# Squares of t summed on ScalarE in nine operations, the low part of h moved to VectorE, and new call orders on four engines

## The reference, cut to what matters

```
x = x + conv_block(ln_over_channels(x))      # 3x3 patches against 512 prototypes
t = tokens(x)                                # 96 channels each
t = t + ffn(ln_t(t))                         # 96 -> 384 -> 96, values rounded to fp8/fp16 steps
ln_t(v) = (v - mean(v)) / sqrt(var(v) + 1e-5)
```

## Time and profile before

| | |
|---|---|
| median of 3 runs | 1996.17 us (1995.54 to 1996.33) |
| the profiled execution | 1996.22 us, of which span 1994.4 us |
| busy, share of the span | PE 95%, DVE 94%, ACT 83%, POOL 81% |
| granted PE clock | 0.985 in the mean, 1.00 from 100 to 1900 us |
| DVE sum of squares (L1041) | 133.4 us in 128 operations |
| ACT squares (L510) | 119.6 us in 128 operations |
| POOL low part of h (L420) | 58.6 us in 128 operations |

### The profile page before, as it was taken

How to read it: one execution, slowest core, us unless ns; L and a number is a source line. 1 busy time by engine, 2 the same in 40 slices (tenths; PEclk the granted TensorE clock), 3 DMA queues, 4 the chain that set the end, 5 groups by cost and what they waited for, 6 DMA issues and landing times.

```text
span 1994.4 us, 44820 instructions
## 1 busy us (share of the span) xinstructions
PE 1898.1 (95%) x13105; PEld 1429.9 (72%) x13105; DVE 1866.6 (94%) x6525; ACT 1656.4 (83%) x3205; POOL 1621.8 (81%) x1170
## 2 busy tenths in 40 slices
PE   5899999999999999999999999999999999999964
PEld 3567777777777777777777777777777777777642
DVE  7999999999999999999999999999999999999740
ACT  1168888888888888888888888888888888888885
POOL 2578888888888888888888888888888888888752
PEclk9999999999999999999999999999999999999985
DMA  3324545454454545445454454544545455454322
GB/s 96 100 73 129 135 125 147 117 147 125 134 139 117 150 122 139 133 127 145 116 147 126 129 143 117 146 126 133 139 119 151 118 143 129 122 150 118 92 74 71
DMA packets 83890, 249.78 MB, mean 125 GB/s; under 512 B 15736, under 2 KB 17986, under 8 KB 83650
## 3 DMA queue, kind: packets, MB, share of 16 engines
q1 hardware_dynamic: 52866, 170.80, 27.3%
q0 software_dynamic: 28672, 75.52, 18.0%
q10 hardware_dynamic: 2112, 0.60, 0.2%
HBM read 133.23 MB, written 57.02 MB: 95 GB/s over the span
## 4 chain that ended last, share of the span: by engine, by line
PE 72%; DVE 10%; issue 6%; ACT 5%; POOL 3%; DMA 2%; POOLq 0%; SPq 0%; ACTq 0%; DVEq 0%
PE y_ps L648 11%; PE y_ps L650 11%; PE y_ps L649 11%; PE bank L673 9%; PE bank L703 8%; PE bank L685 6%; PE bank L739 4%; ACT y L475 4%; PE bank L754 3%; PE bank L713 3%; DVE best_y L1025 3%; PE bank L723 2%; POOL prod L390 2%; DMA wsel<-proto_rows,w_index 1%; PE bank L711 1%
## 5 line engine op out<-in xcount | busy, mean ns | idle before, releaser
L475 ACT CAST y<-bank 128x384 f16<-128x384 f32 x1152 | 554.1, 481 | 185.9 <-PE bank L673 175.4
L1025 DVE TENSOR_REDUCE best_y<-y_ps 128x2 f32<-128x1024 f32 (+1 forms) x640 | 704.6, 1102 | 0.6 <-PE y_ps L650 0.6
L648 PE MATMUL y_ps<-proto_hi,xh 96*128 96x512 f32 x1152 | 574.1, 498 | 22.5 <-DVE best_y L1025 15.1
L483 ACT ACTIVATE h<-y,f_b 128x1152 f16<-128x1152 f16 x384 | 471.7, 1270 | 0.0
L649 PE MATMUL y_ps<-proto_lo,xh 96*128 96x512 f32 x1152 | 456.5, 396 | 0.0
L650 PE MATMUL y_ps<-proto_hi,xl 96*128 96x512 f32 x1152 | 455.9, 396 | 0.0
L673 PE MATMUL bank<-tqt,f_w 96*128 96x384 f16 x1152 | 390.2, 339 | 42.4 <-ACT y L475 34.7
L411 POOL TENSOR_TENSOR xl<-xc,xh 96x1152 fp32r<-96x1152 f32 x128 | 341.2, 2666 | 26.4 <-ACT xh L538 15.5
L343 POOL DMA_INDIRECT xsel<-x_pm,x_index x128 | 121.6, 950 | 230.0 <-DVE xn L983 216.4
L673 PEld LDWEIGHTS bank<-tqt,f_w 96*128 96x128 f16 x1152 | 110.9, 96 | 262.9 <-issue 144.4
L648 PEld LDWEIGHTS y_ps<-proto_hi,xh 96*128 96x128 f32 x1152 | 221.7, 192 | 84.1 <-issue 39.7
(11 more groups left out here) (131 smaller groups left out, 3874.7 us busy)
## 6 DMA issues: line engine op xcount, KB each, us to landing
xc<-x_cm SPq DMA_DIRECT2D x128, 432.0 KB
xp<-x_pm SPq DMA_DIRECT2D x128, 432.0 KB, 5.4
h<-h POOLq DMA_DIRECT2D x128, 432.0 KB, 4.5
out<-o_pm SPq DMA_DIRECT2D x128, 432.0 KB
xsel<-x_pm,x_index POOLq DMA_INDIRECT x128, 3.7
wsel<-proto_rows,w_index POOLq DMA_INDIRECT x128
proto_rows<-proto SPq DMA_DIRECT2D x1, 384.0 KB, 2.7
proto<-w_mask SPq DMA_DIRECT2D x1, 192.0 KB, 3.3
```

The lines of the kernel that those rows point to most:

```text
L475: act.copy(y16[:, q, r * TOK:(r + 1) * TOK], bank[0][:, 0:TOK]).then_inc(s_y16, 1)
L483: act.activation(h16[:, q, :], y16[:, q, :], ACT.Relu, bias=f1_b[:, q:q + 1]).then_inc(s_h16, 1)
L648: pe.matmul(y, hi, proto_hi[:], start=True, stop=False)
L1025: dve.tensor_reduce(best_y[t % 2][:, j0:j1], y_ps[n % 2][:, 0:j1 - j0, :], AX_X, ALU.max).then_inc(s_yd, 1)
```

## The change

Two pieces of work change engine, and the call orders of PE, ACT, DVE and POOL are new. ACT now squares position by position, in nine operations of 128x96 with an accumulator output each, so `t_squares`, `t_sq` and one semaphore go. `low_h` (113x128) moves from POOL to DVE and runs one slot later in stage terms (CONV in place of HIDDEN), at the head of the slot. POOL's `hidden8` moves behind `t_norm`.

```diff
-            def squares(s):
+            def squares(s, js):
                 if run.live(s, CONV):
                     t = s - CONV
-                    act.wait_ge(s_dev, t + 1)
-                    run.wait(s_sqd, t)
-                    run.apart()
-                    act.activation(t_sq[:], t_dev[t % 2][:], ACT.Square).then_inc(s_sq, 1)
+                    for j in js:
+                        if j == 0:
+                            act.wait_ge(s_dev, t + 1)
+                            run.wait(s_rt, s - MATCH)
+                            run.apart()
+                        ins = act.activation(sq_junk[:, j * C:(j + 1) * C], t_dev[t % 2][:, j * C:(j + 1) * C],
+                                             ACT.Square, accum_out=va[(s + 1) % 2][:, J + j:J + j + 1])
+                    if js[-1] == J - 1:
+                        ins.then_inc(s_sq, 1)
...
-            def t_squares(s):
-                if run.live(s, NORM):
-                    dve.wait_ge(s_sq, s - NORM + 1)
-                    ins = dve.tensor_reduce(va[s % 2][:, J:2 * J], t_sq[:].rearrange("p (j c) -> p j c", c=C), AX_X, ALU.add)
-                    ins.then_inc(s_sqd, 1)
...
+            def low_h(s):
+                if run.live(s, CONV):
+                    t = s - CONV
+                    dve.wait_ge(s_h1h, t + 1)
+                    run.wait(s_cv, 2 * t)
+                    dve.tensor_tensor(h1l[:], h1f[:, 0, :], h1h[:, 0, :].bitcast(F32), ALU.subtract).then_inc(s_h1l, 1)
```

More of the change, by code:

```diff
@@ L117, in build @@
         mean_t = [sb(f"mean_t{b}", [P, J]) for b in range(2)]
-        t_sq = sb("t_sq", [P, JC])
+        sq_junk = sb("sq_junk", [P, JC])
         va = [sb(f"va{b}", [P, 4 * J]) for b in range(2)]
@@ L205, in build @@
         s_mean = sem("mean_t_ready")
-        s_sq = sem("t_sq_ready")
-        s_sqd = sem("t_sq_summed")
+        s_sq = sem("sq_t_ready")
         s_rest = sem("rest_ready")
@@ L412, in low_x @@
                                        ALU.subtract).then_inc(s_xl, 1)
[L414 to L420, removed]
             def gather_w(s):
@@ L435, in slot @@
                 gather_x(s)
-                hidden8(s)
                 lock(s)
                 t_norm(s)
+                hidden8(s)
                 t_center(s)
@@ L442, in slot @@
                 output(s)
-                low_h(s)
                 gather_w(s)
@@ L567, in slot @@
             def slot(s):
+                ffn1_out(s, 0)
                 hidden16(s, FFN2, 2)
-                ffn1_out(s, 0)
+                ffn1_out(s, 1)
                 vcs_out(s)
-                ffn1_out(s, 1)
+                high(s)
                 ffn1_out(s, 2)
                 xnt_out(s)
-                high(s)
+                weighted(s)
+                layer1_out(s)
                 ffn1_out(s, 3)
-                mix_out(s)
[L577 to L581, removed]
+                turned(s, 0)
+                ffn1_out(s, 4)
+                squares(s, range(0, 2))
+                squares(s, range(2, 4))
+                ffn1_out(s, 5)
+                mix_out(s)
+                squares(s, range(4, 7))
+                ffn1_out(s, 6)
+                squares(s, range(7, 9))
                 turned(s, 1)
+                ffn1_out(s, 7)
                 hidden1_out(s)
-                ffn1_out(s, 6)
-                squares(s)
-                ffn1_out(s, 7)
                 hidden16(s, FFN, 0)
                 ffn2_out(s, 0)
+                ffn2_out(s, 1)
                 ffn1_out(s, 8)
-                ffn2_out(s, 1)
                 hidden16(s, FFN, 1)
@@ L759, in slot @@
                 match(s, 0)
+                hidden2(s)
+                ffn1(s, 0)
                 match(s, 1)
-                ffn1(s, 0)
-                hidden2(s)
                 conv(s, 0)
+                ffn1(s, 1)
                 match(s, 2)
-                ffn1(s, 1)
+                conv(s, 1)
+                ffn1(s, 2)
                 turn_x(s)
+                layer1(s)
                 match(s, 3)
-                ffn1(s, 2)
-                conv(s, 1)
                 ffn1(s, 3)
+                turn(s, 0)
+                match(s, 4)
+                ffn1(s, 4)
+                match(s, 5)
                 turn_mix(s)
[L772 to L777, removed]
                 ffn1(s, 5)
                 match(s, 6)
+                match(s, 7)
+                ffn1(s, 6)
+                turn(s, 1)
+                pick(s)
+                ffn1(s, 7)
                 hidden1(s)
[L781 to L784, removed]
                 match(s, 8)
                 ffn2(s, 0)
+                ffn2(s, 1)
                 ffn1(s, 8)
-                ffn2(s, 1)
             run.slots(slot)
@@ L953, in variances @@
                     if run.live(s, NORM):
-                        dve.wait_ge(s_sqd, s - NORM + 1)
+                        dve.wait_ge(s_sq, s - NORM + 1)
                         run.apart()
@@ L1078, in slot @@
             def slot(s):
-                t_squares(s)
                 low_part(s)
-                mix_sims(s)
[L1082 to L1087, removed]
+                x_dif(s)
+                low_h(s)
+                cos(s)
+                x_sq(s)
+                x_sum(s)
+                x_norm(s)
+                mix_sims(s)
                 variances(s)
@@ L1090, in slot @@
                 root(s, 0)
+                mix_row(s)
                 one_hot(s)
@@ L1097, in slot @@
                 root(s, 3)
+                ffn2_bias(s)
                 root(s, 4)
-                residual(s, 0)
                 root(s, 5)
                 pick_root(s)
-                ffn2_bias(s)
                 root(s, 6)
-                y_max(s, 0)
+                residual(s, 0)
+                remainder(s)
                 residual(s, 1)
                 t_mean(s)
-                remainder(s)
+                y_max(s, 0)
                 y_max(s, 1)
@@ L1111, in slot @@
                 y_max(s, 2)
+                sims(s)
+                y_max(s, 3)
+                best_v(s)
                 x_stats(s, [5])
+                v_index(s)
                 x_stats(s, [6, 7, 8])
[L1114 to L1117, removed]
                 y_max(s, 4)
```

## The result

The changed kernel takes 2028.84 us in the median of four runs (2028.66 to 2030.73), against 1995.86 for the kernel before (1994.62 to 1996.33, four runs). The ratio is 1.0168 with a 95% interval of 1.0151 to 1.0186: 33 us slower, or 1.7%. I had forecast 1982 with a range up to 2022.

A forecast was written before the change was run, and what follows sets the result against it. PE's list, waits included, was taken as the bound: 14.32 - 0.06 + 0.05 + 0.15 + 0.02 + 0.02 = 14.50 a slot against 14.605. Over 120 slots that saves 12.6 us, the drain 1 to 2 more: 1982 us, range 1962 to 2022.

The forecast's parts named there:

- PE's work of 14.32 a slot: PE's list in a full slot: 14.55 undisturbed less 0.23 lost waiting for ACT's copy out of bank 0.
- the wait at `match 4`: New PE wait, as match 4 needs y_max(0), now behind residual(1) and t_mean: 0.1 to 0.25, taken as 0.15.
- both stop being near the bound, and neither gain counts in itself: DVE falls from 14.37 to 13.6 a slot and POOL loses 0.45 of 12.59; neither gain counts in itself.
- With `t_mean` ready at 5.8 it now reaches the gather at 13.9: POOL reaches gather_w 8.0 after t_mean is ready, leaving 6.5 us until weighted in the next slot.
- x: Spacing of one of ACT's nine squares with its accumulator read: bounds 0.19 to 0.56, taken as 0.24.
- The analogy with DVE's read: ACT's accumulator read taken as 0.05, near DVE's, where the next instruction starts together with the read.
- Rival 1: ACT becomes the bound because the accumulator read does not overlap: slower, 2021 us or 2065; chance 0.28.
- the break of 0.275: Square spacing on ACT above which PE's next hidden2 waits for ffn2_out(1); every 0.01 more adds 0.09 a slot.
- the 14.4 that I had named as a sign of being wrong: ACT busy over 14.4 of the slot would show the prediction wrong; ACT was forecast at 14.2.
- The other sign: PE waiting for ACT ahead of hidden2, expected if the squares' spacing is over 0.28.
- late `wsel` rows: ACT's weighted waiting for gather_w's rows: a 1 us stall in one of ten slots, counted as 0.02 on average.
- the drain 1 to 2 shorter: In the drain, where ACT's squares and DVE's sum stood one after the other, the change saves 1 to 2 us.

The follow-up runs named there:

- the version of 1988 us: Changed kernel with x_stats(5) and x_stats(6-8) ahead of sims, weighted behind turned(0), and y_max(0) ahead of residual(1) and t_mean: 1988.42 us, ratio 0.9968 to the kernel before.
- the version with the loop opened: Changed kernel with only x_stats(5) and x_stats(6-8) moved ahead of sims on DVE: 2015.77 us, ratio 1.0103 to the kernel before.

## Why the prediction was wrong

The span came out 46.5 us longer than forecast. In the full slots I had 12.6 us less and it is 17.0 more, which makes 29.6; at the two ends I had 1.4 less and it is 15.5 more, which makes 16.9. Point 2 is the first part, point 6 the second.

1. **What bounds the kernel.** PE did set the time before, though only just: the loop stood at 14.4 beneath its 14.55. PE's work of 14.32 a slot roughly held. Without the wait at `match 4` my sum gives 14.35, and the version of 1988 us, which has no such wait, has calm slots of 14.39.
2. **DVE and POOL, "both stop being near the bound, and neither gain counts in itself".** This is the step that failed. Their loads came out near what I had worked (DVE 13.83 against 13.6, POOL 12.31 against 12.14), but load was the wrong measure. The one place where I put POOL in time is "With `t_mean` ready at 5.8 it now reaches the gather at 13.9": it has `t_center` start as soon as `t_mean` is done, as if POOL were free. In the trace POOL is still in its list (`gather_x`, `t_norm`, `hidden8`), and `t_center` starts 1.14 later; counted from `match 0` (1013.62) the gather that I had at 13.9 comes at 15.5 (1029.10). I never closed the circle: `sims` to `xn` on DVE, `gather_x` to `product` on POOL, `sims` again. It was 14.4 before and became 14.70, which sets the slot in place of the 14.50 that I had from PE. Shown by undoing the squares (+0.97 for 0.96 put in), by `low_h` on POOL (-0.17 for 0.20 taken out), by the statistics moved out (wait at `sims` gone) and by POOL's order alone (+0.48 for a wait of 0.49). In the prediction `gather_x` had no time at all, though it takes 1.07 and ends 0.38 later than `root(6)`.
3. **ACT and x.** Taken as 0.24 (0.19 for the square, 0.05 for the read), measured 0.266 (0.174 and 0.093), in the bounds of 0.19 to 0.56; the square alone came out under the 0.19. The analogy with DVE's read was wrong: on ACT the read has a spacing of 0.09 of its own, so ACT became 1.56 a slot heavier where I had 1.33. Rival 1, my main case for slower, had the right sign by another cause: x stayed under the break of 0.275, and ACT 0.84 lighter left the slot as it was. Only with the nine squares in a block, in the old orders, has ACT a large share of the chain (30%). ACT was busy 14.35 of the slot, just under the 14.4 that I had named as a sign of being wrong. The other sign came: PE waits for ACT ahead of `hidden2`, 0.18 a slot. But it points at the wrong engine, as the run with the reads left out shows; with the statistics moved ahead and ACT's work unchanged that spacing is 0.23 again.
4. **The wait at `match 4`.** Forecast 0.15, there with 0.12, and 0.12 came off when it was removed in the version where PE bound. The mechanism and the size were right, and the calm slot of the version with the loop opened (14.50 to 14.54) is the 14.50 that I gave. In the changed kernel it cost nothing, because the loop was longer.
5. **Transfers.** I counted 0.02 a slot for late `wsel` rows. In the changed kernel ACT waits 4.8 us for them in all; once the loop was opened, they cost 0.10 a slot.
6. **Fill and drain.** I had the drain 1 to 2 shorter and nothing on start and fill. Measured: +8.2 for the drain and +7.3 for the other two. In the drain ACT's squares no longer hide behind anything: 4 to 5 us (4.0 with the reads left out, 3.7 with the single operation, 4.7 with two squares). The rest goes with the new orders: with the squares undone the drain is 123.4, where it is 118.7 in the old orders, and PE's and ACT's order alone adds 12.0, POOL's 2.5, DVE's 1.7. The clock was at half speed more often too. That is in part a result of waiting: with the nine squares in a block in the old orders PE's list is as before, and yet 92.8 us of the drain are at 1.2 GHz against 57.6. How much of the longer drain the lower clock in turn makes stays open. The two windows show ACT busier and PE's clock lower:

```profile
1875.50:1994.40 118.90, 70.92 (x516) 48.14 (x514) 36.81 (x128) 87.83 (x164) 55.45 (x44) 0.76 0.28 75
```

```profile
1900.00:2026.90 126.90, 78.69 (x520) 55.23 (x520) 38.02 (x126) 98.10 (x267) 54.35 (x39) 0.69 0.26 70
```

The first is the kernel before, the second the changed one; the third figure from the end is the granted clock (0.76 and 0.69). The fill's 5.4 comes neither from the squares alone (109.2 in the old orders, against 110.6) nor from `low_h` alone (111.4). With the squares undone and all orders new it is 119.4, in slots that are also 0.97 longer than the changed kernel's. So it goes with the new orders, and which of them makes it is not shown.

## What to carry to other kernels

Where several engines are nearly full, sum the loops of dependences between them, not only each engine's load: start at one instruction, follow what it waits for through each in-order list until you are back one iteration later, and compare that length with the slot. Work moved to an engine that is not full costs its full length if it lands inside the loop that sets the time, and an edit that is worth nothing in the shadow of a loop (`y_max(0)` here) can be worth 0.7% once the loop is opened. Count the thin slots at both ends apart from the full ones, since what hides in the full slots stands in the open there.

## What the runs showed of the hardware

- An ACT operation with an accumulator output is two instructions here: for 96 columns 0.17 and 0.09 us from start to start. On DVE the read took 0 to 0.03.
- A small DVE instruction with both inputs in SBUF took 1.07 in place of 0.27 us when it began beside a GpSimd tensor operation (the kernel with `gather_x` behind `product`). Beside POOL's gather instruction it stayed at 0.27.
- PE's granted clock was at 1.2 GHz for 3.4 us of the fill and 57.6 of the drain before, and 20.5 and 78.4 after. With PE's list as before and only the squares changed, in a block, it was 6.8 and 92.8: what other engines make PE wait moves the clock as well.
